# Quantising w_down in the attention stage of a gated cross-attention block, and transposing it by DMA from DRAM

## The chip, the cores and the metric

The kernel runs on one core of one Trainium2 chip. The metric is the device time of one execution in microseconds (us), as the median over runs: lower is better. Engines are named as in the profile: PE is TensorE's matmul, PEld its weight load, DVE VectorE, ACT ScalarE, POOL GpSimd, SP SyncE (which here only issues DMAs).

## What is computed

The block takes x (2 x 2048 x 512, f32) and a context of 2 x 77 x 384, and computes

```
x = x + tanh(g_xattn) * (softmax(q k^T * scale) v) Wo          # 16 heads of 32, q from layernorm(x)
xq = act_fake_quant(layernorm(x), clip_x)                      # one scale for the whole tensor
h = act_fake_quant(silu(xq wq(w_gate)^T) * (xq wq(w_up)^T), clip_down)   # 1408 hidden columns
x = x + tanh(g_ffn) * (h wq(w_down)^T)                         # w_down is 512 x 1408

wq(w) = clip(round(w / s), -128, 127) * s,  s = max(|w|, axis=1) / 127   # one scale per row of w
```

What matters here is the last weight. Row r of w_down (one of 512) gets its own scale, its 1408 values become int8, and these small integers are exact in bf16. TensorE needs them the other way round, with the 1408 hidden indices on the partitions: the tile `wdT`, 128 x 11 x 512 in bf16.

## The kernel before, in words

The 4096 rows of x are 32 tiles of 128 rows. Three stages (blocks) follow each other, with a barrier of all engines between them.

**Attention** is written as slots (`tile_slots`, 36 of them, slots 4 to 19 in a hardware loop). In slot n every engine runs a fixed order of pieces that belong to neighbouring tiles: scores of tile n, probabilities and outputs of tile n-1, the output projection (`project`) of tile n-2, the second layer norm of tile n-3, queries of tile n+2, the transpose of tile n+4 and so on. In slots 0 to 21 each slot also takes one block of 128 rows of w_gate or w_up (`NW` is 22): SP loads it into `w_in` (`rows`, line 323), DVE takes the absolute maximum (L632), its reciprocal (L641) and the int8 values (L649), POOL casts them to bf16 in `w_bf` (L404), and SP brings them transposed into `wgu` with a DMA transpose from SBUF to SBUF (`rows_transposed`, L316). After slot 21 SP has nothing left to do in this stage. The order on DVE inside a slot is: maximum of the first half of the scores (L570), residual add (L609), subtraction (L576), statistics (L623), low part of the transposed output (L599), then the piece of the weights (L632), `bn_aggr` (L635), outputs (L584, L589), second half of the scores (L570), int8 weights (L649), subtraction (L576), `xmax` (L659), low part of the queries (L555), outputs, statistics of tile n+6 and the low part of the transposed x (L548). PE's transpose of the output two tiles back (L846, `out_transpose`) waits for that low part (L548) of the slot before.

**Up** computes the hidden activations in 8 groups of 512 rows. A group has 11 steps (u counts them, 88 in all); a step is four matmuls of 128x512 for the gate and four for up (L1235), a silu on ACT (L1120), a product on DVE (L1192) and a maximum of it (L1196). The quantised inputs of the next group are made by ACT (L1095), cast by POOL (L1089) and transposed by SP's DMA transposes into `xqT` (L1064), four tiles to a group; `xqb`, the source, has two buffers, and POOL waits for the transpose of two tiles back before it writes one again. After a group is done, SP stores h of groups 0 to 3 to DRAM (`h_spill`, L1072, 2816 KB each) from the same queue.

In the first two groups every engine also has a piece of w_down. SP loads it as four blocks of 128 rows into the part of `h` that group 3 uses (L1057). In step u, `wd_step(u)` gives the block r (five steps each) and its phase k: DVE takes maxima (L1162), the scale (L1167, L1169, L1170) and int8 chunks of 512, 512 and 384 columns (L1177); ACT casts a chunk to bf16 one step later (L1106); PE transposes it, 4, 4 and 3 times 128x128, after the matmuls of a step (L1245); ACT copies the result from PSUM to `wdT` (L1112).

```
c = wd_chunk(u - 2) if isinstance(g, int) and g < 2 else None
if c is not None:
    pe.wait_ge(a_wdb, c + 1)          # ACT's cast of chunk c
    if c >= 2:
        pe.wait_ge(a_wdT, c - 1)      # ACT's copy of chunk c-2
```

**Down** multiplies the quantised h by `wdT`, 11 matmuls of 128x512 for each of 32 tiles (L1406).

Of the kernel before, what the change touches and what calls it, by code (L numbers as in the profile page):

```python
# [15 lines left out]
P = 128  # L16
# [35 lines left out]

CHUNKS = [(0, 4), (4, 8), (8, 2 * KB)]


def flamingo_block(nc, x, ctx_in, mask, g_xattn, g_ffn, Wq, Wk, Wv, Wo, clip_x, clip_down,
# [3 lines left out]
    h_spill = nc.dram_tensor("h_spill", [NS * TG, P, KI * P], F32, kind="Internal").ap()  # L60

    top = ExitStack()
    with top:
# [29 lines left out]
        with attn:  # L93
# [17 lines left out]
            with work:  # L111
# [26 lines left out]
                w_inv = sb("w_inv", [P, 1])  # L138

# [107 lines left out]
                v_wi8 = sem("v_wi8")  # L247
                a_xhi = sem("a_xhi")
# [61 lines left out]
                def _(sp):  # L310
# [218 lines left out]
                def _(dve):  # L529
# [70 lines left out]

                    def slot(n, t):
# [27 lines left out]
                        if runs(n, NW):  # L629
# [3 lines left out]
                               .then_inc(v_wam, 1)  # L633
                        if runs(m, NT):
# [11 lines left out]
                        if runs(n, NW):  # L646
# [3 lines left out]
                               .then_inc(v_wi8, 1)  # L650
                        if runs(n, NT):
# [5 lines left out]
                        if runs(n - 4, NT):  # L657
                            wait(dve, a_abs, n - 3)
                            dve.tensor_reduce(xmax[:, span(n - 4)], xabs[:, :], X, ALU.max).then_inc(v_xmax, 1)  # L659
                        if runs(n + 2, NT):  # L660
# [301 lines left out]
        with ffn:  # L962
# [10 lines left out]
            with up:  # L973
# [11 lines left out]
                wd_am = sb("wd_am", [P, KD, WC])  # L985
                wd_max = sb("wd_max", [P, KD])
                wd_inv = sb("wd_inv", [P, KD])
                wd_i8 = [sb(f"wd_i8{i}", [P, D], I8) for i in range(2)]
                wd_bf = [sb(f"wd_bf{i}", [P, D], BF16) for i in range(2)]

                wd_raw = h[:, (NS - 1) * TG:NS * TG, :, :].rearrange("p t k n -> p t (k n)")
                p_w = [pb(f"w{i}", [P, 2 * KD, P], BF16) for i in range(2)]
                l_wd = [sem(f"l_wd{i}") for i in range(KD)]
                v_wd = sem("v_wd")
                v_wd8 = sem("v_wd8")
                a_wdb = sem("a_wdb")
                t_wd = sem("t_wd")
                a_wdT = sem("a_wdT")
# [28 lines left out]
                def wd_cols(q):  # L1027
                    return slice(q * D, min(q * D + D, I))

                def wd_step(u):  # L1030
                    r, k = divmod(u, WC + 2)
                    return (r, k) if isinstance(u, int) and 0 <= r < KD else (None, None)

                def wd_chunk(u):

                    r, k = wd_step(u)
                    return r * WC + k - 2 if r is not None and k >= 2 else None

# [16 lines left out]
                def _(sp):  # L1055
                    for r in range(KD):
                        sp.dma_start(wd_raw[:, r, :], w_down[r * P:(r + 1) * P, :]).then_inc(l_wd[r], 16)  # L1057
                    def tiles_transposed(g):
                        if g >= 2:
                            sp.wait_ge(t_u, KI * (g - 1))  # L1060
                        for t in range(TG):
# [3 lines left out]
                              .then_inc(d_xqT[n % 2], 16)  # L1065

                    for g in range(1, NG):
                        tiles_transposed(g)
                        if g <= NG - NS:
# [4 lines left out]
                              .then_inc(h_out[f], 16)  # L1074
                    for i in range(2):
# [16 lines left out]
                def _(act):  # L1092
# [5 lines left out]
                    def down_part(u):  # L1098

                        c = wd_chunk(u - 1)  # L1100
                        if c is not None:
                            n = wd_cols(c % WC).stop - wd_cols(c % WC).start
                            act.wait_ge(v_wd8, c + 1)
                            if c >= 2:
                                act.wait_ge(t_wd, c - 1)
                            act.copy(wd_bf[c % 2][:, 0:n], wd_i8[c % 2][:, 0:n]).then_inc(a_wdb, 1)  # L1106
                        c = wd_chunk(u - 3)
                        if c is not None:
                            r, q = divmod(c, WC)
                            n = (wd_cols(q).stop - wd_cols(q).start) // P  # L1110
                            act.wait_ge(t_wd, c + 1)
                            act.copy(wdT[:, 4 * q:4 * q + n, r * P:(r + 1) * P], p_w[c % 2][:, 0:n, :])\  # L1112
                               .then_inc(a_wdT, 1)

                    def group(g, j, slot):
                        for i in range(KI):
# [7 lines left out]
                            if isinstance(g, int) and g < 2:  # L1124
                                down_part(u)
                        if isinstance(g, int) and g == 1:
                            down_part(2 * KI)
# [10 lines left out]
                def _(dve):  # L1138
# [16 lines left out]
                    def down_part(u):  # L1155
                        r, k = wd_step(u)
                        if r is None:
                            return
                        if k < 2:
                            dve.wait_ge(l_wd[r], 16)  # L1160
                            for q in ((0, 1), (2,))[k]:
                                dve.tensor_reduce(wd_am[:, r, q:q + 1], wd_raw[:, r, wd_cols(q)], X, ALU.max,  # L1162
                                                  apply_absolute_value=True).then_inc(v_wd, 1)
                        steps = (WC + 3) * r + WC
                        if k == 1:
                            dve.wait_ge(v_wd, steps)
                            dve.tensor_reduce(wd_max[:, r:r + 1], wd_am[:, r, :], X, ALU.max).then_inc(v_wd, 1)  # L1167
                            dve.wait_ge(v_wd, steps + 1)
                            dve.reciprocal(wd_inv[:, r:r + 1], wd_max[:, r:r + 1]).then_inc(v_wd, 1)  # L1169
                            dve.tensor_scalar(swd[:, r:r + 1], wd_max[:, r:r + 1], 1.0 / QMAX, None, ALU.mult)\  # L1170
                               .then_inc(v_wd, 1)
                        if k >= 2:
                            c, cols = wd_chunk(u), wd_cols(k - 2)
                            dve.wait_ge(v_wd, steps + 3)
                            if c >= 2:
                                dve.wait_ge(a_wdb, c - 1)
                            dve.tensor_scalar(wd_i8[c % 2][:, 0:cols.stop - cols.start], wd_raw[:, r, cols],  # L1177
                                              wd_inv[:, r:r + 1], QMAX, ALU.mult, ALU.mult).then_inc(v_wd8, 1)

                    def group(g, j, slot):  # L1180
# [6 lines left out]
                        for i in range(KI):  # L1187
# [10 lines left out]
                            if isinstance(g, int) and g < 2:  # L1198
                                down_part(u)
# [234 lines left out]
```

## Time and profile before

| | us |
|---|---|
| median of 3 runs (660.31 to 660.74) | 660.56 |
| the profiled execution, its own time | 660.23 |
| its span, from the first to the last instruction | 658.4 |
| attention, until the up stage's first instruction | 406.2 |
| up, from the first to the last start of four L1235 matmuls | 413.4 to 570.5 |
| down, from its first L1406 matmul to the end | 577.8 to 658.4 |

PE is busy 97% of the span, DVE 76%, ACT 50%, POOL 25%. The profile gives for each engine the start and length of its instructions, what ended the idle time ahead of them, and the clock that TensorE was granted. Matmuls overlap, so the length of one (379 ns) is not the time it costs; the distance between starts is. The row that a view prints for a run of the same matmuls begins with the start of the first.

### The profile page before, as it was taken

How to read it: one execution, taken by the hardware profiler on the slowest of the kernel's cores; microseconds unless marked ns; L12 is line 12 of the kernel's file. 1: busy time of each engine (PE TensorE's matmuls, PEld its weight loads, DVE VectorE, ACT ScalarE, POOL GpSimd, SP SyncE). 2: the span in 40 equal slices, each digit the busy share in tenths (PEclk: the TensorE clock that was granted, in tenths of full speed). 3: DMA queues.
4: the chain of work that ended last, by engine and by line, in shares of the span. 5: the costliest groups of instructions: out<-in, count | busy, mean ns of one | idle time of the engine just before them, and what ended most of it. 6: DMA issues, size and time to landing. Idle time of an engine off the chain costs nothing. (4 is left out here: it accounts for less than half of the span.)

```text
span 658.4 us, 12936 instructions
## 1 busy us (share of the span) xinstructions
PE 636.1 (97%) x4018; PEld 478.7 (73%) x4018; DVE 502.8 (76%) x942; ACT 330.7 (50%) x509; POOL 167.3 (25%) x378
## 2 busy tenths in 40 slices
PE   8979999999999999999999996999999999899997
PEld 6779999999999999999999994444444444444443
DVE  6687788787878878777776665899888888866664
ACT  5254545444554544445454344667555554265553
POOL 7121213232232323211100111111111110057775
PEclk9989999999999999999999997999999999999999
DMA  8739111111010101000000002343565110089623
GB/s 304 188 110 295 49 25 50 24 31 41 24 48 24 48 24 40 18 1 1 1 2 1 1 1 98 102 183 78 165 209 201 30 24 17 0 321 399 270 109 114
DMA packets 51079, 60.45 MB, mean 92 GB/s; under 512 B 33475, under 2 KB 33629, under 8 KB 51037
## 3 DMA queue, kind: packets, MB, share of 16 engines
q1 hardware_dynamic: 46131, 43.15, 21.8%
q10 hardware_dynamic: 4906, 16.78, 6.9%
q8 instruction: 22, 0.36, 0.2%
q14 instruction: 20, 0.16, 0.1%
HBM read 32.48 MB, written 19.92 MB: 80 GB/s over the span
## 5 line engine op out<-in xcount | busy, mean ns | idle before, releaser
L570 DVE TENSOR_REDUCE sb_smax<-ps_s 128x8 f32<-128x616 f32 x64 | 51.1, 799 | 66.7 <-PE ps_s L801 66.5
L1235 PE MATMUL ps_g<-sb_xqT,sb_wgu 128*128 128x512 bf16 x352 | 90.4, 379 | 0.6 <-DVE sb_xqT L1203 0.5
L1235 PE MATMUL ps_u<-sb_xqT,sb_wgu 128*128 128x512 bf16 x352 | 90.3, 379 | 0.0
L1120 ACT ACTIVATE sb_silu<-ps_g,sb_sgu 128x512 f32<-128x512 f32 x88 | 60.5, 687 | 59.2 <-PE ps_g L1235 30.9
L464 ACT COPY sb_pT<-ps_p 128x512 f32<-128x512 f32 (+1 forms) x96 | 46.4, 520 | 70.6 <-PE ps_p L812 70.6
L823 PE MATMUL ps_o<-sb_vblk,sb_pT 128*128 (+4 forms) x640 | 79.0, 270 | 1.2 <-ACT sb_pT L464 1.2
L823 PEld LDWEIGHTS ps_o<-sb_vblk,sb_pT 128*128 128x128 f32 (+1 forms) x640 | 76.8, 191 | 1.8 <-ACT sb_pT L464 1.4
L756 PE MATMUL ps_q<-sb_xT_hi,sb_wq_hi 128*128 128x256 f32 x256 | 77.5, 303 | 0.0
L1192 DVE SCALAR_TENSOR_TENSOR sb_h<-ps_u,sb_sgu,sb_silu 128x512 f32<-128x512 f32 (+1 forms) x88 | 65.9, 749 | 14.9 <-PE ps_u L1235 13.1
L1406 PE MATMUL ps_z<-sb_wdT,sb_hq 128*128 128x512 bf16 x352 | 76.4, 380 | 0.0
L758 PE MATMUL ps_q<-sb_xT_hi,sb_wq_lo 128*128 128x256 f32 x256 | 72.3, 282 | 0.0
L757 PE MATMUL ps_q<-sb_xT_lo,sb_wq_hi 128*128 128x256 f32 x256 | 72.2, 282 | 0.0
L1318 POOL TENSOR_TENSOR sb_wgu<-sb_wgu,sb_x 128x512 f32<-128x512 f32 x31 | 53.9, 1737 | 53.2 <-DVE sb_wgu L1363 53.2
L1196 DVE TENSOR_REDUCE sb_hmax<-sb_h 128x1 f32<-128x512 f32 (+1 forms) x88 | 60.4, 686 | 7.6
L1406 PEld LDWEIGHTS ps_z<-sb_wdT,sb_hq 128*128 128x128 bf16 x352 | 34.4, 98 | 42.3 <-ACT sb_hq L1333 0.8
L1235 PEld LDWEIGHTS ps_u<-sb_xqT,sb_wgu 128*128 128x128 bf16 x352 | 34.4, 98 | 41.5 <-DVE sb_h L1192 0.5
L452 ACT CAST sb_oT_hi<-ps_x 128x512 fp32r<-128x512 f32 x31 | 18.2, 586 | 90.7 <-PE ps_x L846 90.7
L1235 PEld LDWEIGHTS ps_g<-sb_xqT,sb_wgu 128*128 128x128 bf16 x352 | 33.8, 98 | 39.5 <-DVE sb_xqT L1203 0.7
L1333 ACT CAST sb_hq<-sb_h 128x1408 bf16<-128x1408 int8 x32 | 43.6, 1365 | 35.1 <-DVE sb_h L1357 35.1
L576 DVE TENSOR_TENSOR sb_prob<-ps_s,sb_smax 128x616 f32<-128x616 f32 x64 | 51.0, 797 | 3.0
L386 POOL TENSOR_TENSOR sb_ve<-sb_mvt,sb_eps 128x1 f32<-128x1 f32 x32 | 6.1, 190 | 180.0 <-DVE sb_mvt L635 180.0
L756 PE MATMUL ps_y<-sb_wo_hi,sb_oT_hi 128*128 128x512 f32 x124 | 51.3, 414 | 0.0
(177 smaller groups left out, 1348.5 us busy)
## 6 DMA issues: line engine op xcount, KB each, us to landing
h_spill<-sb_h SPq DMA_DIRECT2D x4, 2816.0 KB, 8.8
sb_h<-h_spill ACTq DMA_DIRECT2D x16, 704.0 KB, 6.5
out_dram<-sb_wgu SPq DMA_DIRECT2D x32, 256.0 KB, 2.1
sb_x<-in_x_dram ACTq DMA_DIRECT2D x1, 4096.0 KB, 18.3
sb_w_in<-in_L_ffn_w_gate_dram SPq DMA_DIRECT2D x11, 256.0 KB, 2.6
sb_w_in<-in_L_ffn_w_up_dram SPq DMA_DIRECT2D x11, 256.0 KB, 2.7
sb_h<-in_L_ffn_w_down_dram SPq DMA_DIRECT2D x4, 704.0 KB, 6.0
sb_x<-in_x_dram SPq DMA_DIRECT2D x2, 1024.0 KB, 14.8
```

The costliest lines, as they stand in the source:

```text
L570: dve.tensor_reduce(smax[:, half, :].rearrange("p (g h) -> p g h", g=2), half_scores(), X, ALU.max).then_inc(v_max, 1)
L576: dve.tensor_tensor(prob[t % 2][:, half, :].rearrange("p (g h m) -> p g h m", g=2, h=HG), half_scores(), smax[:, half, :].rearrange("p (g ...
L756: pe.matmul(o, hi, rhi, start=first, stop=False)
L757: pe.matmul(o, hi, rlo, start=False, stop=False)
L758: return pe.matmul(o, lo, rhi, start=False, stop=last)
L823: last = pe.matmul(p_o[:, first:end + 1, :].rearrange("p h d -> p (h d)"), pT[rows, half * KB + j, :], vblk[rows, span(b), half, SLOT0[j]: ...
L1120: act.activation(silu[(j * KI + i) % 2][:, :, :].rearrange("p t n -> p (t n)"), p_g[(j * KI + i) % 2][:, :], ACT.Silu, scale=sgu[:, i:i + ...
L1192: dve.scalar_tensor_tensor(steps_h, p_u[(j * KI + i) % 2][:, :, :], sgu[:, KI + i:KI + i + 1], silu[(j * KI + i) % 2][:, :, :], ALU.mult, ...
L1196: dve.tensor_reduce(hmax[:, span(u)], steps_h, mybir.AxisListType.XY, ALU.max, apply_absolute_value=True).then_inc(v_hmax, 1)
L1235: last = pe.matmul(banks[(j * KI + i) % 2][:, :], wgu[:, what, k, i * P:(i + 1) * P], xqT[j][:, k, :], start=(k == 0), stop=(k == KD - 1))
L1318: pool.tensor_tensor(yd[k], yd[k], x1[:, span((v + RT) % NT), :].rearrange("p a d -> p (a d)"), ALU.add).then_inc(g_out, 1)
L1406: last = pe.matmul(p_z[k % 4][:, :], hq[k % 4][:, i, :], wdT[:, i, :], start=(i == 0), stop=(i == KI - 1))
```

## The change

w_down leaves the up stage. In attention slots 22 to 29 two slots go to each block r of 128 rows: in the even one DVE takes the three maxima and the scale, in the odd one it makes the int8 chunks. POOL casts chunks 0 and 1 in the odd slot and chunk 2 in the next one, into the one buffer `w_bf`, and SP stores each to `wd_spill` in DRAM. The raw rows lie in `w_in`, in a new tile `w_in2` and in `vblk` of batch 0, which is free once that batch's outputs are done (`t_o`). In the up stage SP issues, after tiles 1 and 3 of groups 1 and 2, one DMA transpose of a 128 x 1408 block from DRAM into `wdT`. The pieces on PE, ACT and DVE of the up stage, the four loads and their PSUM tiles are gone.

```diff
+    wd_spill = nc.dram_tensor("wd_spill", [KD, P, I], BF16, kind="Internal").ap()
...
+                w_in2 = sb("w_in2", [P, I - 2 * D])
+                vb0 = vblk[:, 0, :, :, :].rearrange("p a s d -> p (a s d)")
+                wd_in = [w_in[:, :], vb0[:, 0:D], w_in2[:, :]]
+                wd_i8 = [w_i8[:, :], vb0[:, D:D + D // 4].bitcast(I8), vb0[:, D + D // 4:D + D // 2].bitcast(I8)]
...
@@ attention, SP, after rows_transposed(NW - 1)
+                    def down_rows(r):
+                        if r:
+                            sp.wait_ge(v_wd8, WC * r)
+                        for q in range(WC):
+                            cols = wd_cols(q)
+                            sp.dma_start(wd_in[q][:, 0:cols.stop - cols.start], w_down[r * P:(r + 1) * P, cols])\
+                              .then_inc(l_wd[r], 16)
+
+                    def down_stored(r, q):
+                        cols = wd_cols(q)
+                        sp.wait_ge(g_wdb, WC * r + q + 1)
+                        sp.dma_start(wd_spill[r, :, cols], w_bf[:, 0:cols.stop - cols.start]).then_inc(d_wdb, 16)
+
+                    sp.wait_ge(t_o, 2 * (S // P))
+                    sp.wait_ge(v_wi8, NW)
+                    down_rows(0)
+                    for r in range(KD):
+                        for q in range(WC - 1):
+                            down_stored(r, q)
+                        if r + 1 < KD:
+                            down_rows(r + 1)
+                        down_stored(r, WC - 1)
                     sp.wait_ge(d_wT, 16 * NW)
+                    sp.wait_ge(d_wdb, 16 * KD * WC)
@@ attention, POOL, at the end of slot(n, t)
+                        for m, parts in ((n - 1, [WC - 1]), (n, range(WC - 1))):
+                            r, k = wd_step(m)
+                            for q in parts if k == 1 else []:
+                                c, size = WC * r + q, wd_cols(q).stop - wd_cols(q).start
+                                pool.wait_ge(v_wd8, c + 1)
+                                wait(pool, d_wdb, 16 * c)
+                                if c == 0:
+                                    pool.wait_ge(d_wT, 16 * NW)
+                                pool.tensor_copy(w_bf[:, 0:size], wd_i8[q][:, 0:size]).then_inc(g_wdb, 1)
@@ attention, DVE: down_part(n, 0) ahead of L635, down_part(n, 1) ahead of the second L576,
@@ down_part(n, 2) and down_scale(n) ahead of L555
+                    def down_part(n, q):
+                        r, k = wd_step(n)
+                        if k == 0:
+                            if q == 0:
+                                dve.wait_ge(l_wd[r], 16 * WC)
+                            dve.tensor_reduce(wd_am[:, r, q:q + 1], wd_in[q], X, ALU.max,
+                                              apply_absolute_value=True).then_inc(v_wdam, 1)
+                        if k == 1:
+                            if q == 0:
+                                dve.wait_ge(v_wds, 3 * r + 3)
+                                dve.wait_ge(g_wbf, NW)
+                                wait(dve, g_wdb, WC * r)
+                            size = wd_cols(q).stop - wd_cols(q).start
+                            dve.tensor_scalar(wd_i8[q][:, 0:size], wd_in[q][:, 0:size], wd_inv[:, r:r + 1], QMAX,
+                                              ALU.mult, ALU.mult).then_inc(v_wd8, 1)
@@ up, SP
-                    for r in range(KD):
-                        sp.dma_start(wd_raw[:, r, :], w_down[r * P:(r + 1) * P, :]).then_inc(l_wd[r], 16)
                     def tiles_transposed(g):
...
                             sp.dma_start_transpose(xqT[g % 2][:, :, t * P:(t + 1) * P], xqb[n % 2][:, :])\
                               .then_inc(d_xqT[n % 2], 16)
+                            if g <= KD // 2 and t % 2:
+                                r = (g - 1) * 2 + t // 2
+                                sp.dma_start_transpose(wdT[:, :, r * P:(r + 1) * P], wd_spill[r]).then_inc(d_wdT, 16)
...
+                    sp.wait_ge(d_wdT, 16 * KD)
@@ up, PE (ACT's down_part with L1106 and L1112, and DVE's with L1162 to L1177, go as well)
-                            c = wd_chunk(u - 2) if isinstance(g, int) and g < 2 else None
-                            if c is not None:
-                                pe.wait_ge(a_wdb, c + 1)
-                                if c >= 2:
-                                    pe.wait_ge(a_wdT, c - 1)
-                                for k in range((wd_cols(c % WC).stop - wd_cols(c % WC).start) // P):
-                                    last = pe.transpose(p_w[c % 2][:, k, :], wd_bf[c % 2][:, k * P:(k + 1) * P],
-                                                        identb[:, :])
-                                last.then_inc(t_wd, 1)
```

`wd_step(n)` in attention gives block `(n - 22) // 2` and phase `(n - 22) % 2`; `down_scale(n)` makes the block's maximum, its reciprocal and `swd` in phase 0, three instructions of one column or three, each waiting for the one before.

## Rows read from the trace of the kernel before

**Rows 1.** Two windows: busy us (count) of PE, PEld, DVE, ACT, POOL; clock, DMA, GB/s
```profile
254.40:265.90 11.50, 11.50 (x88) 10.98 (x87) 9.38 (x20) 5.77 (x10) 2.88 (x11) 1.00 0.15 36
413.40:457.40 44.00, 41.51 (x220) 19.01 (x220) 40.88 (x78) 30.53 (x53) 4.91 (x8) 1.00 0.36 102
```

**Rows 2.** Timeline of PE, attention (start us, us, then engine, line, operation, count)
```profile
254.38 0.30 PE L799 MATMUL ps_s<-sb_k_hi,sb_q_hi 128*128 128x308 f32 x1
255.24 0.60 PE L846 MATMUL ps_x<-sb_identf,sb_o_sb 128*128 128x128 f32 x4
265.89 0.30 PE L799 MATMUL ps_s<-sb_k_hi,sb_q_hi 128*128 128x308 f32 x1
...
288.90 0.30 PE L799 MATMUL ps_s<-sb_k_hi,sb_q_hi 128*128 128x308 f32 x1
300.40 0.30 PE L799 MATMUL ps_s<-sb_k_hi,sb_q_hi 128*128 128x308 f32 x1
```

**Rows 3.** Timeline of PE, up stage
```profile
413.36 1.04 PE L1235 MATMUL ps_g<-sb_xqT,sb_wgu 128*128 128x512 bf16 x4 [0.52 <-DVE sb_xqT L1203]
...
422.72 0.40 PE L1245 MATMUL ps_w<-sb_identb,sb_wd_bf 128*128 128x128 bf16 x4 [0.55 <-ACT sb_wd_bf L1106]
422.95 1.03 PE L1235 MATMUL ps_g<-sb_xqT,sb_wgu 128*128 128x512 bf16 x4
...
424.90 1.03 PE L1235 MATMUL ps_g<-sb_xqT,sb_wgu 128*128 128x512 bf16 x4
...
457.42 1.03 PE L1235 MATMUL ps_g<-sb_xqT,sb_wgu 128*128 128x512 bf16 x4
...
569.66 1.03 PE L1235 MATMUL ps_g<-sb_xqT,sb_wgu 128*128 128x512 bf16 x4
```

**Rows 4.** Timeline of DVE, attention, slot 20 (it has a weight block)
```profile
258.77 0.68 DVE L632 TENSOR_REDUCE sb_w_am<-sb_w_in 128x1 f32<-128x512 f32 x1
...
260.87 0.48 DVE L649 TENSOR_SCALAR sb_w_i<-sb_w_in,sb_w_inv 128x512 int8<-128x512 f32 x1
...
264.16 0.68 DVE L548 TENSOR_TENSOR sb_xT_lo<-ps_x,sb_xT_hi 128x512 fp32r<-128x512 f32 x1
```

**Rows 5.** Timeline of DVE, up stage, the pieces of block 0
```profile
416.69 1.27 DVE L1162 TENSOR_REDUCE sb_wd_am<-sb_h 128x1 f32<-128x512 f32 x2
417.88 0.74 DVE L1192 SCALAR_TENSOR_TENSOR sb_h<-ps_u,sb_sgu,sb_silu 128x512 f32<-128x512 f32 x1
...
419.25 0.54 DVE L1162 TENSOR_REDUCE sb_wd_am<-sb_h 128x1 f32<-128x384 f32 x1
...
420.15 0.74 DVE L1192 SCALAR_TENSOR_TENSOR sb_h<-ps_u,sb_sgu,sb_silu 128x512 f32<-128x512 f32 x1
```

**Rows 6.** Timeline of SP's queue: the last weight transpose, two input transposes of up
```profile
273.75 1.19 SPq L316 DMA_TRANSPOSE sb_wgu<-sb_w_bf  x1
...
419.98 1.19 SPq L1064 DMA_TRANSPOSE sb_xqT<-sb_xqb  x1
...
464.04 2.11 SPq L1064 DMA_TRANSPOSE sb_xqT<-sb_xqb  x1
```

**Rows 7.** All of L1064: issue ns min/median/max, time to landing; loads of the page
```profile
L1064 SPq DMA_TRANSPOSE sb_xqT<-sb_xqb x28: 1189/1192/2729, 416.6 to 546.9; - x28
...
DMA to landing us min/median/max: 2.4/2.5/8.3
...
sb_w_in<-in_L_ffn_w_up_dram SPq DMA_DIRECT2D x11, 256.0 KB, 2.7
```

**Rows 8.** DMA of 270 to 280 us (one transpose): packets, MB, share of 16 engines
```profile
q1 hardware_dynamic: 544, 0.13, 6.7%
```

**Rows 9.** DMA of 262 to 264.45 us (one 256 KB load, one transpose), same columns
```profile
q1 hardware_dynamic: 688, 0.39, 64.7%
```

**Rows 10.** PE between up and down: us, busy (x), granted clock, DMA share, GB/s
```profile
575.00:576.00 1.00, 1.00 (x6) 0.53 0.00 0
...
578.00:579.00 1.00, 1.00 (x5) 0.77 0.91 338
```

More of the change, by code:

```diff
@@ L51, with wd_cols, wd_step @@
 ROWS = [min(P, HW - P * k) for k in range(KB)]
+WD0 = 2 * KI
+def wd_cols(q):
+    return slice(q * D, min(q * D + D, I))
+def wd_step(n):
+    r, k = divmod(n - WD0, 2) if isinstance(n, int) else (-1, 0)
+    return (r, k) if 0 <= r < KD else (None, None)
 CHUNKS = [(0, 4), (4, 8), (8, 2 * KB)]
@@ L138, in flamingo_block @@
                 w_inv = sb("w_inv", [P, 1])
+                wd_am = sb("wd_am", [P, KD, WC])
+                wd_max = sb("wd_max", [P, KD])
+                wd_inv = sb("wd_inv", [P, KD])
+                w_in2 = sb("w_in2", [P, I - 2 * D])
+                vb0 = vblk[:, 0, :, :, :].rearrange("p a s d -> p (a s d)")
+                wd_in = [w_in[:, :], vb0[:, 0:D], w_in2[:, :]]
+                wd_i8 = [w_i8[:, :], vb0[:, D:D + D // 4].bitcast(I8), vb0[:, D + D // 4:D + D // 2].bitcast(I8)]
                 p_s = pb("s", [P, 2, 512])
@@ L247, in flamingo_block @@
                 v_wi8 = sem("v_wi8")
+                l_wd = [sem(f"l_wd{r}") for r in range(KD)]
+                v_wdam = sem("v_wdam")
+                v_wds = sem("v_wds")
+                v_wd8 = sem("v_wd8")
+                g_wdb = sem("g_wdb")
+                d_wdb = sem("d_wdb")
                 a_xhi = sem("a_xhi")
@@ L599, in out_part, with down_scale @@
                         dve.tensor_tensor(o_lo, p_x[:, :, :], o_hi.bitcast(F32), ALU.subtract).then_inc(v_olo, 1)
+                    def down_part(n, q):
[13 more added lines that the diff above has]
+                                              ALU.mult, ALU.mult).then_inc(v_wd8, 1)
+                    def down_scale(n):
+                        r, k = wd_step(n)
+                        if k == 0:
+                            dve.wait_ge(v_wdam, WC * (r + 1))
+                            dve.tensor_reduce(wd_max[:, r:r + 1], wd_am[:, r, :], X, ALU.max).then_inc(v_wds, 1)
+                            dve.wait_ge(v_wds, 3 * r + 1)
+                            dve.reciprocal(wd_inv[:, r:r + 1], wd_max[:, r:r + 1]).then_inc(v_wds, 1)
+                            dve.tensor_scalar(swd[:, r:r + 1], wd_max[:, r:r + 1], 1.0 / QMAX, None, ALU.mult)\
+                               .then_inc(v_wds, 1)
                     def slot(n, t):
@@ L633, in slot @@
                                .then_inc(v_wam, 1)
+                        down_part(n, 0)
                         if runs(m, NT):
@@ L650, in slot @@
                                .then_inc(v_wi8, 1)
+                        down_part(n, 1)
                         if runs(n, NT):
@@ L659, in slot @@
                             dve.tensor_reduce(xmax[:, span(n - 4)], xabs[:, :], X, ALU.max).then_inc(v_xmax, 1)
+                        down_part(n, 2)
+                        down_scale(n)
                         if runs(n + 2, NT):
@@ L984, in flamingo_block @@
                 sgu = sb("sgu", [P, 2 * KI])
[L985 to L998, printed above, removed]
+                d_wdT = sem("d_wdT")
                 rsq = sb("rsq", [P, NT])
@@ L1022, in flamingo_block @@
                 v_hmax = sem("v_hmax")
[L1027 to L1037, printed above, removed]
                 def groups(eng, group):
@@ L1123, in group @@
                                 quantise(g * TG + TG + i // 2, i // 2)
[L1124 to L1127, printed above, removed]
                     act.activation(warm[:, :], eps[:, :], ACT.Silu).then_inc(a_warm, 1)
@@ L1153, in _ @@
                     dve.wait_ge(v_sx, 5)
[L1155 to L1178, printed above, removed]
                     def group(g, j, slot):
@@ L1197, in group @@
                                               apply_absolute_value=True).then_inc(v_hmax, 1)
-                            if isinstance(g, int) and g < 2:
-                                down_part(u)
                     def place(n):
```

15 lines of the change are left out of this document (removed).

## The prediction

> **What bounds the kernel now.** I read the windows first. In a slot of the attention stage PE is busy for all 11.50 us and DVE for 9.38; in groups 0 and 1 of the up stage PE is busy for 41.5 of 44 us, DVE for 40.9 [rows 1]. So PE sets the pace in both places, and the second is the only long stretch in which it has gaps. Whether PE is bound by itself or by someone it waits for is read from its timeline, from the distance between starts.
>
> Attention: the first scores matmul of slot 20 starts at 254.38, of slot 21 at 265.89, of slot 23 at 288.90, of slot 24 at 300.40 [rows 2]. Which slot is which follows from SP: the last of 22 weight transposes is issued at 273.75, so that slot is number 21 [rows 6]. A slot takes 11.50 us with a weight block and without one. DVE's and POOL's share of the weight costs nothing there; that cover is what the change leans on.
>
> Up: group 2 starts at 457.42 and its last step's gate at 569.66, 65 steps later [rows 3]. That is 1.7268 us a step, eight matmuls of 216 ns, with no room in between. The first 22 steps should take 22 x 1.7268 = 37.99 us; they take 457.42 - 413.36 = 44.06. **The w_down pieces cost PE 6.07 us**, and PE is the bound behind them, so this is on the path. One gap shows what it is made of: the four transposes start at 422.72 after 0.55 us of idle time that ACT's cast ends, the gate matmuls follow at 422.95, and the next chunk, whose cast is ready, makes the step 424.90 - 422.95 = 1.95 us, 0.22 more than a plain one [rows 3]. The rest is waiting for ACT, which waits for DVE.
>
> **The change, part by part.**
>
> Removed from PE: the transposes and the waits ahead of them, 6.07 us, all of it. What is late next in groups 0 and 1? DVE: its 40.9 us [rows 1] lose the w_down pieces. They take 1.19 us for two maxima (416.69 to 417.88) and 0.90 for the third and the scale (419.25 to 420.15) [rows 5], and three int8 chunks of up to 0.48 each, as L649 takes [rows 4]: about 3.5 us a block, 14 in all. 27 us are left for 38 us of PE. ACT also loses work. So the pace becomes that of group 2 onward, which the trace shows PE holding for 65 steps. I take the whole 6.07.
>
> Added to DVE in attention, even slots 22 to 28: 1.19 + 0.90 = 2.09 us [rows 5], against 0.68 + 0.48 = 1.16 and a small reciprocal in a slot with a weight block [rows 4]. That is some 0.9 us more than DVE is known to hide. Who waits? The tightest is PE's L846 in the next slot, 0.86 us after that slot's start (255.24 - 254.38) [rows 2], so at 266.75 for slot 21; it needs L548 of slot 20, which ends at 264.16 + 0.68 = 264.84 [rows 4]. The slack is 1.9 us; 0.9 goes, 1.0 is left. Odd slots add three int8 chunks, at most 1.44 us, 0.3 above a weight slot: hidden. In the last two slots, 28 and 29, DVE has less of its own to do. POOL has 2.88 of 11.5 us busy [rows 1]; its two casts in a slot and its wait for each store queue only the layer norm of a later tile behind them. Cost nothing; the bounds are nothing and, if every one of the eight slots lost the 0.3 us by which my estimates could err, 2.4 us.
>
> The loads: SP issues block 0 after 273.75 + 1.19 = 274.94; three loads at 2.7 us to landing each [rows 7], three in a row at most 8. DVE wants them in slot 22, whose start is 265.89 + 11.50 = 277.39, at the place of L632, 258.77 - 254.38 = 4.39 us into it: 281.8 [rows 2, 4]. Landed by then, by 283 at the worst, and L548's slack covers the 1.2. Later blocks have more: SP issues them when the odd slot's chunks are done. The twelve stores and the wait for them end some 30 us before the stage does. Nothing.
>
> Gone from the start of up: four loads of 704 KB that nobody waited for in time. Nothing.
>
> **The four DMA transposes** are the unknown. No row shows a source in DRAM or 1408 columns. Issue on SP: 1.19 us for 512 columns [rows 7], so between 1.19 (if it is a fixed price) and, with the longest that a busy queue makes of it (2.73), 2.73 x 2.75 = 7.5 us; I take 1.19 x 2.75 = 3.3, the uncontended rate. Transfer: 6.7% of 10 us = 0.67 us for 512 columns [rows 8], so 1.84 us from below. From above: a 256 KB load and a transpose together take 64.7% of 2.45 us = 1.59 [rows 9], so the load's 128 packets take 0.92 us, 115 ns each on one of 16 engines; were each of the 1408 pieces as slow, 88 x 0.115 = 10.1 us. I take about 2.5, near the transposes' own row.
>
> One rule of the Trainium skill says that this is a bargain: by "Advanced Engine Details and Errata", section "X-Bar Transpose (TRN2)", a DMA transpose is as fast as a plain DMA, 350 to 400 GB/s. By that estimate the 360 KB would take 1.0 us; the trace speaks against it, 0.131 MB in 0.67 us is 196 GB/s [rows 8], and the sum goes by the row.
>
> What stands behind them? SP's queue is in order, so tiles 2 and 3 of the same group are issued after the first of the pair. Group 0: tile 1's issue ends at 419.98 + 1.19 = 421.17 [rows 6]; with X for the issue of a block, tiles 2 and 3 need 1.19 each and 1.3 more to land (2.5 in all [rows 7]), 421.17 + X + 3.68. Group 1 now starts at 413.36 + 11 x 1.7268 = 432.36. Free up to X = 7.5. Group 1: here the 2.8 MB store of h goes through the same queue. The pattern of group 2, undisturbed by w_down, gives tile 1's issue ended 464.04 + 2.11 - 457.42 = 8.73 us after the start [rows 3, 6], so 12.41 + X against 19.0: free up to X = 6.6. With X = 3.3 the slack is 4.2 and 3.3 us. Blocks 1 and 3 follow tile 3 and end before the next store is due. Nothing.
>
> **Down.** The granted clock is 0.5 of full, the 1.2 GHz level, from 575.06 to 578.46 [rows 10], after the pause between the stages. The down matmuls start at 577.83, so 0.63 us at half speed cost 0.3. Moved by 6 us, the stretch may miss them (0.3 less) or fall wholly on them (3.4 / 2 = 1.7, 1.4 more). I put nothing into the sum.
>
> **Sum.** Profiled execution: 660.23 - 6.07 = 654.16, span 652.4. The median shown stands 0.33 above that execution, so 660.56 - 6.07 = **654.5**.
>
> **Rivals.**
> (a) *The transposes from DRAM hold up the input tiles a little.* X between 6.6 and 8, or their transfer in the upper half of its bounds. For it: in group 1 the queue is already slow (2.11, 2.73, a landing of 8.3 us [rows 6, 7]). Against: X would be over twice the rate of the rows. It gives back 1 to 4 us: 655.5 to 658.5.
> (b) *They hold it up much*: the slower side. The mechanism is SP's queue. Four blocks in a row delay tiles, then the store of h, then group 2's tiles: with X the tiles of group 2 land at 432.0 + 3X (block 0, tiles 2 and 3, block 1, store, tiles 0 and 1 at 2.2 each, block 2, tiles 2 and 3), against 451.4. That is 3X - 19.4 late, and eats the 6.07 from X = 8.5 us on; at X = 10, the same as the upper bound of the transfer, it is 10.6 late: 665.1. A sentence of the Trainium skill points that way: "DMA: Bandwidth & Descriptors", section "Why small descriptors are slow (HBM only)", says that short descriptors pay on HBM and not between SBUF tiles. The rows here show only the SBUF kind [rows 8].
> (c) *DVE's even slots overrun.* If maxima and scale take 1 us longer than in up, or the loads come late, L846 waits: four to eight slots by 0.3 us, 655.7 to 656.9. Against: 1.0 us of slack.
> (d) *The low clock falls on the down stage*: 655.9.
> (e) *Nothing moves*: another engine holds groups 0 and 1 at 2 us a step. Against it stand the 65 steps after them. 660.5.
>
> **How the numbers follow.** Forecast 0.70; (a) 0.07, (b) 0.08, (c) 0.06, (d) 0.06, (e) 0.03. A measurement of this kernel tells 0.2%, 1.3 us, from no change. All but (b) and (e) are faster: 0.89; (e) is the same, 0.03; (b) slower, 0.08. The range goes from 653.6 (the clock's 0.3 and the scatter of the runs, 0.4, below the sum) to 657.2, which takes in (c), (d) and half of (a): 0.15 lies outside.
>
> **What would show it.** Group 1's gate should start 19.0 us after group 0's and group 2's 38.0 us after, no L1245 or L1106 in up; slots 22 to 27 keep 11.50 us and 28 and 29 their length; L548 in even slots about 1 us later. Block transposes: issue near 3.3 us, landing within 6. The prediction is wrong if PE idles ahead of group 1 or 2 for a transpose, or if a slot of 22 to 29 is longer than before.

## The result, and the profile after

The changed kernel takes 655.62 us (median of 7 runs, 652.95 to 657.17) beside 660.7 us of the kernel before (7 runs, 658.95 to 662.6) on the same chip: ratio 0.992, 95% interval 0.9894 to 0.9945. A second measurement gave 653.86 us (6 runs) beside 660.23 (11 runs), ratio 0.9902 [0.9882, 0.9921]. The forecast was 654.5 in 653.6 to 657.2: faster, and both medians are inside. The profiled execution of after took 652.95 us with a span of 651.1, that of before 660.23 and 658.4. The difference of 7.28 us is 6.06 in groups 0 and 1 of the up stage, 1.01 ahead of it (413.36 - 412.35), and 0.2 behind.

Four windows of the changed kernel: a slot of attention that takes the maxima and the scale of a w_down block (slot 22), a slot that makes the int8 chunks (23), the first two groups of the up stage, and groups 2 on. [rows 1] has a slot and the two groups of the kernel before. Columns: us, busy us (count) of PE, PEld, DVE, ACT, POOL; granted clock; DMA share; GB/s.

```profile
276.33:287.84 11.51, 11.51 (x87) 10.99 (x86) 10.25 (x23) 5.76 (x10) 1.34 (x6) 1.00 0.11 38
287.84:299.34 11.50, 11.50 (x87) 10.98 (x86) 9.77 (x22) 5.77 (x10) 3.64 (x13) 1.00 0.12 32
412.35:450.35 38.00, 38.00 (x177) 17.23 (x178) 30.17 (x42) 20.69 (x30) 4.90 (x8) 1.00 0.57 142
450.35:563.50 113.15, 113.15 (x526) 51.30 (x525) 94.03 (x131) 58.68 (x86) 12.27 (x20) 1.00 0.31 100
```

DVE took on work in attention, 10.25 of 11.51 us busy where [rows 1] has 9.38, and PE is still busy for the whole slot. In up, DVE's count is 42 where it was 78, and PE has no gap left in 38.00 us. The starts behind it, from PE's timeline of the up stage:

```profile
412.35 1.04 PE L1258 MATMUL ps_g<-sb_xqT,sb_wgu 128*128 128x512 bf16 x4 [0.52 <-DVE sb_xqT L1226]
...
431.35 1.03 PE L1258 MATMUL ps_g<-sb_xqT,sb_wgu 128*128 128x512 bf16 x4
...
450.35 1.03 PE L1258 MATMUL ps_g<-sb_xqT,sb_wgu 128*128 128x512 bf16 x4
```

Group 1 begins 19.00 us and group 2 38.00 us after group 0, where [rows 3] have 44.06 for the second. This is one execution; in a second profiled execution of the same kernel the 38.00 are 39.28 (below, on the clock). The blocks arrive through SP's queue. Its timeline in the up stage (start us, issue us), and then all four of L1135 and all 28 of L1131, the input's transposes, with issue ns min/median/max:

```profile
418.97 1.19 SPq L1131 DMA_TRANSPOSE sb_xqT<-sb_xqb  x1
420.21 1.42 SPq L1135 DMA_TRANSPOSE sb_wdT<-wd_spill  x1
...
427.11 1.44 SPq L1135 DMA_TRANSPOSE sb_wdT<-wd_spill  x1
432.33 0.40 SPq L1142 DMA_DIRECT2D h_spill<-sb_h  x1
434.55 5.52 SPq L1131 DMA_TRANSPOSE sb_xqT<-sb_xqb  x2
440.12 2.82 SPq L1135 DMA_TRANSPOSE sb_wdT<-wd_spill  x1
444.15 2.50 SPq L1131 DMA_TRANSPOSE sb_xqT<-sb_xqb  x2
446.70 1.45 SPq L1135 DMA_TRANSPOSE sb_wdT<-wd_spill  x1
```

```profile
L1135 SPq DMA_TRANSPOSE sb_wdT<-wd_spill x4: 1422/1444/2821, 420.2 to 446.7; - x4
...
DMA to landing us min/median/max: 3.6/3.7/4.8
```

```profile
L1131 SPq DMA_TRANSPOSE sb_xqT<-sb_xqb x28: 1189/1191/2177, 415.6 to 539.8; - x28
```

A block costs SP 1.42 us, hardly more than the 1.19 of an input tile with 2.75 times fewer columns: nearly a fixed price. Only the third, issued some 8 us behind the 2.8 MB store of h, costs twice that, 2.82. The last input tile that is issued during group 1 is issued by 446.65, and group 2, which reads it, starts at 450.35.

In attention the question was L611, the subtraction of the low part of x that PE waits for in the next slot. DVE's timeline at the end of slot 22, and PE's around the start of slot 23:

```profile
284.71 0.54 DVE L669 TENSOR_REDUCE sb_wd_am<-sb_w_in 128x1 f32<-128x384 f32 x1
...
287.21 0.68 DVE L611 TENSOR_TENSOR sb_xT_lo<-ps_x,sb_xT_hi 128x512 fp32r<-128x512 f32 x1
...
288.89 0.80 DVE L633 TENSOR_REDUCE sb_smax<-ps_s 128x8 f32<-128x616 f32 x1 [0.91 <-PE ps_s L894]
```

```profile
287.84 0.30 PE L892 MATMUL ps_s<-sb_k_hi,sb_q_hi 128*128 128x308 f32 x1
...
288.69 0.38 PE L939 MATMUL ps_x<-sb_identf,sb_o_sb 128*128 128x128 f32 x2
```

L611 ends at 287.89 and PE comes to L939 at 288.69: 0.8 us are left, and DVE still sits idle for 0.91 us afterwards. Every slot from 22 to 27 lasts 11.50 us and slots 28 and 29 last 11.1, as before.

### The profile page after: what moved, and what is told of

It reads as the page before. It is cut to its first block and busy times, and to the rows that moved or that the text cites. A ratio compares the mean times of both kernels' runs of the same rounds, so it can differ in the third digit from the quotient of the medians.

```text
span 651.1 us, 12848 instructions
## 1 busy us (share of the span) xinstructions
PE 630.8 (97%) x3974; PEld 475.6 (73%) x3974; DVE 502.3 (77%) x942; ACT 320.0 (49%) x485; POOL 173.7 (27%) x390
```

## The experiments

Ten kernels ran, in three batches; the kernel before took 660.2, 660.37 and 660.23 us in them (medians of 22, 25 and 11 runs). Eight take the change apart, the others repeat it and extend it. Times are medians.

**What held groups 0 and 1 back.** The prediction put the 6.07 us on PE's transposes and on PE's wait for ACT's cast. In the kernel before, this edit moves the transposes of a chunk between the gate and the up matmuls of the next step, 0.86 us later:

```
 last.then_inc(done, 1)
+if what == 0 and isinstance(g, int) and g < 2:
+    down_chunk(wd_chunk(u - 3))       # was wd_chunk(u - 2), after the step
```

> The kernel before, with PE's w_down transposes moved from the end of a step to between the next step's gate and up matmuls, 0.86 us later. Nothing else is changed. Theory (6.07 us are 2.4 us of PE work and 3.6 us of waiting for ACT's cast, which was up to 0.64 us late): the waits go, the work stays, group 2 starts 38.0 + 2.4 = 40.4 us after group 0 and the kernel takes about 656.9, 3.6 less than before. Rival (the whole 6.07 is the price of the transposes' work on PE, switching included): group 2 still starts 44 us after group 0, 660.5.

Measured: 660.63 us (10 runs), ratio 1.0007 [0.9989, 1.0025]. Groups 0 and 1 take 457.54 - 413.50 = 44.04 us, as before. PE's timeline in the up stage, two of its gaps:

```profile
431.20 0.39 PE L1246 MATMUL ps_u<-sb_xqT,sb_wgu 128*128 128x512 bf16 x1 [0.38 <-DVE sb_h L1192]
...
441.30 0.39 PE L1246 MATMUL ps_u<-sb_xqT,sb_wgu 128*128 128x512 bf16 x1 [0.38 <-DVE sb_h L1192]
```

These gaps of PE were not closed, they became waits for DVE's h, which frees the PSUM bank. The two stand 10.10 us apart, five steps at 2.02 us. The theory of the wait for ACT fell. The new one: DVE, busy 40.9 of 44 us [rows 1], sets the pace, and whoever PE asks next is late. DVE's timeline of the kernel before bears it out. The pairs of maxima that open blocks 1 and 2:

```profile
426.79 1.27 DVE L1162 TENSOR_REDUCE sb_wd_am<-sb_h 128x1 f32<-128x512 f32 x2
...
436.89 1.27 DVE L1162 TENSOR_REDUCE sb_wd_am<-sb_h 128x1 f32<-128x512 f32 x2
```

With that of block 0 at 416.69 [rows 5] they are 10.10 us apart, and from its first h at 415.30 until 457.5 DVE's timeline shows no idle time ahead of any instruction. Two kernels each keep one half. The first is the changed kernel with PE's transposes and ACT's copies put back, but with blocks loaded ready from DRAM, so that DVE has no work for w_down in up and ACT has no casts:

```
-    sp.dma_start_transpose(wdT[:, :, r * P:(r + 1) * P], wd_spill[r])
+    sp.dma_start(wd_raw[:, r, 0:I], wd_spill[r])           # at the start of up, r = 0..3
+    last = pe.transpose(p_w[c % 2][:, k, :], wd_raw[:, c // WC, q * P:(q + 1) * P], identb[:, :])
+    act.copy(wdT[:, 4 * q:4 * q + n, r * P:(r + 1) * P], p_w[c % 2][:, 0:n, :])
```

> The changed kernel, but w_down comes back from DRAM with four plain loads and is transposed as before by PE (44 transposes after the steps of groups 0 and 1, L1245 of the kernel before) and copied by ACT. So PE and ACT have their work of before in up, and DVE has none. Theory after e1 (DVE is what paces groups 0 and 1 before the change: 10.1 us for every five steps; PE's own work is 44 transposes of 55 ns): group 2 starts 38.0 + 2.4 = 40.4 us after group 0, the kernel takes 2.4 us more than the changed one, about 657 to 658. Rival (the transposes cost PE the whole 6.07): 44 us, 660 to 661.

Measured: 656.64 us (10 runs), ratio 0.9945 [0.9926, 0.9964]. PE's timeline at both ends of groups 0 and 1:

```profile
413.82 1.04 PE L1278 MATMUL ps_g<-sb_xqT,sb_wgu 128*128 128x512 bf16 x4 [0.52 <-DVE sb_xqT L1246]
...
454.28 1.03 PE L1278 MATMUL ps_g<-sb_xqT,sb_wgu 128*128 128x512 bf16 x4
```

The distance is 40.46 us, so PE's transposes alone, with ACT's copies, cost 2.46. The other half is the kernel before without PE's transposes, ACT's casts and its copies; DVE's pieces stay, and wdT holds zeros, so the down product is left out of the output.

```
-    act.copy(wd_bf[c % 2][:, 0:n], wd_i8[c % 2][:, 0:n])
-    last = pe.transpose(p_w[c % 2][:, k, :], wd_bf[c % 2][:, k * P:(k + 1) * P], identb[:, :])
-    dve.wait_ge(a_wdb, c - 1)
+    pool.memset(wdT[:, n - TG, :], 0.0)                    # eleven small pieces
```

> The kernel before with DVE's w_down pieces in up, and without PE's transposes and ACT's casts and copies; GpSimd fills wdT with zeros between its casts, so the output is not the reference's. Theory (DVE paces groups 0 and 1): group 2 starts 42.5 to 44 us after group 0, against 44.06 before, and the kernel stays at 659 to 660.5, although all of PE's part is gone. Rival (the cost is PE's and ACT's): 38.0 us, about 654.5.

Measured: 659.02 us (10 runs), ratio 0.9972 [0.9954, 0.999]. The window of groups 0 and 1 (columns as above), one of PE's gaps, and two pairs of DVE's maxima:

```profile
413.40:457.40 44.00, 40.05 (x177) 16.27 (x180) 40.98 (x78) 20.71 (x30) 8.52 (x16) 1.00 0.38 108
```

```profile
429.71 1.04 PE L1231 MATMUL ps_u<-sb_xqT,sb_wgu 128*128 128x512 bf16 x4 [0.65 <-DVE sb_h L1188]
```

```profile
437.83 1.27 DVE L1160 TENSOR_REDUCE sb_wd_am<-sb_h 128x1 f32<-128x512 f32 x2
...
447.93 1.27 DVE L1160 TENSOR_REDUCE sb_wd_am<-sb_h 128x1 f32<-128x512 f32 x2
```

Groups 0 and 1 take 456.61 - 413.94 = 42.67 us: with nothing of w_down on PE or ACT they are still 4.67 us too long, DVE is busy for 40.98 us, and its blocks are 10.10 us apart as in the kernel before. (Some 0.35 us of the 4.67 are the filling's own: one int8 chunk, at 423.89, took 0.83 us instead of 0.48 beside a fill of POOL.) 2.46 and 4.67 make 7.13, more than the 6.06 of both: they overlap. Taking off PE's and ACT's work only would have saved 1.4 us, taking off DVE's, and with it ACT's casts, only 3.6.

**Do the additions cost anything?** The changed kernel without any of the w_down work (loads, maxima, casts, stores, block transposes); the down product is again left out.

```
-    down_part(n, 0)   (and 1, 2, down_scale, down_rows, down_stored, the casts)
-    sp.dma_start_transpose(wdT[:, :, r * P:(r + 1) * P], wd_spill[r])
+    pool.memset(wdT[:, :, :], 0.0)
```

> The changed kernel with everything of w_down left out: no loads, maxima, int8, casts, stores or block transposes; wdT is filled with zeros and swd with ones by GpSimd at the start of up, so the output is not the reference's. Theory (all that the change adds is hidden): the same as the changed kernel on the same chip, within its scatter of 653 to 657, slots 22 to 29 of 11.50 and 11.1 us, group 2 starts 38.0 us after group 0. Rival (the additions in attention or the block transposes cost something that the gain covered): faster by over 1 us, slots 22 to 29 shorter than the changed kernel's.

Measured: 659.69 us (10 runs), ratio 0.9986 [0.9968, 1.0004], slower than the changed kernel with all its work. The fill that should have cost nothing spoiled the run. Timelines of POOL, DVE and PE at the start of up:

```profile
405.97 4.79 POOL L1114 MEMSET sb_wdT<- 128x5632 bf16 x1
...
406.10 4.74 DVE L1153 TENSOR_SCALAR sb_spread<-sb_identf,sb_am 128x128 f32<-128x128 f32 x1
...
410.98 0.55 PE L1235 MATMUL ps_u<-sb_spread,sb_ones 128*128 128x128 f32 x1 [4.11 <-DVE sb_spread L1153]
```

DVE's small instruction lasted as long as POOL's fill (in the next kernel, without that fill beside it, it took 0.28 us), and up began at 417.34 instead of near 413. So it was done again with the fill in eleven pieces between POOL's casts, `pool.memset(wdT[:, n - TG, :], 0.0)`:

> e2 again with the filling of wdT cut in 11 pieces between GpSimd's casts (in e2 the one fill of 4.8 us held up DVE at the start of up). w_down is left out altogether; the output is not the reference's. Theory: the same as the changed kernel, 653 to 657, group 2 starts 38.0 us after group 0. Rival: the additions cost something, and it is faster than 652.5.

Measured: 655.5 us (5 runs), ratio 0.9931 [0.9904, 0.9959]. Up starts at 413.43, group 2 at 451.43: 38.00 us. The changed kernel, with all the work, has ratios of 0.992 and 0.9902: no difference that the runs can show, and its slots and its 38.00 us are the same. What it adds is hidden.

How well, is asked by two more. The maxima of the even slots are taken twice, 1.64 us more of DVE in each:

```
 dve.tensor_reduce(wd_am[:, r, q:q + 1], wd_in[q], X, ALU.max, apply_absolute_value=True)
+dve.tensor_reduce(wd_am2[:, r, q:q + 1], wd_in[q], X, ALU.max, apply_absolute_value=True)
```

> The changed kernel with each of the maxima of slots 22, 24, 26 and 28 taken twice, 1.7 us more of DVE in each of these slots. The trace of the changed kernel has 0.9 us of idle time left on DVE at the end of slot 22. Theory (the slack of the even slots is about 0.8 to 0.9 us): slots 22, 24 and 26 are longer by 0.6 to 1 us each, 28 by less since it has less other work, PE idle ahead of L939's transpose for L611; 2 to 3 us in all. Rival (DVE's queue has more give than that, since the lateness is made up in the odd slots): every slot keeps 11.50 us.

Measured: 657.45 us (7 runs), ratio 0.9945 [0.9927, 0.9963]. PE's timeline at the start of slot 23 and of slot 24, PE's waits from 200 to 400 us (us in total, times, longest), and DVE's timeline at the same start:

```profile
287.68 0.30 PE L895 MATMUL ps_s<-sb_k_hi,sb_q_hi 128*128 128x308 f32 x1
...
289.19 0.63 PE L942 MATMUL ps_x<-sb_identf,sb_o_sb 128*128 128x128 f32 x4 [0.49 <-issue]
...
299.86 0.30 PE L895 MATMUL ps_s<-sb_k_hi,sb_q_hi 128*128 128x308 f32 x1
```

```profile
PEld ps_x L942 <- DVE sb_o_sb L653: 1.4, 2, 0.7
```

```profile
288.41 0.68 DVE L612 TENSOR_TENSOR sb_xT_lo<-ps_x,sb_xT_hi 128x512 fp32r<-128x512 f32 x1
```

Slot 23 lasts 12.18 us, and so does 25 (323.54 - 311.36); slot 27 is 0.26 longer, slot 29 not at all: 1.6 us together where 2 to 3 were expected. 1.64 added, 0.68 of it came through in slots 23 and 25: the slack was 0.96 us. PE's transpose (L942) waits for two pieces of DVE, the outputs (L653) and the low part of x (L612). The view puts the wait down to L653, but that one ends at 288.49; L612 ends at 289.09, and PE goes on at 289.19. It is the instruction that the prediction named, L548 there. Next, the queue. In a copy of the changed kernel the block after tile 1 is transposed again and waited for each time, so that SP is held for about 8 us in each of the two groups; a further kernel does it three times, about 12 us:

```
 sp.dma_start_transpose(wdT[:, :, r * P:(r + 1) * P], wd_spill[r]).then_inc(d_wdT, 16)
+if t == 1:
+    for e in range(1):                                     # range(2) in the second
+        sp.wait_ge(d_wdT, ...)
+        sp.dma_start_transpose(wdT[:, :, r * P:(r + 1) * P], wd_spill[r]).then_inc(d_wdT, 16)
+    sp.wait_ge(d_wdT, ...)
```

> The changed kernel with SP's queue held up on purpose: after tile 1 of groups 1 and 2 the block is transposed twice and SP waits for the landing of each, so the time between tile 1 and tile 2 is X = 7.4 us (2 x 3.7) in group 0's time and about 8.5 us in group 1's, in place of 1.4 and 2.8. Theory (the input tiles are late from X = 7.5 us in group 0 and 6.6 in group 1): group 1 on time or 0.1 us late, group 2 about 1.5 to 2 us late, PE idle ahead of it for a transpose. Rival (POOL's buffers or ACT, not SP's queue, set when the tiles land): PE has no gap at all.

Measured: 656.51 us (5 runs), ratio 0.9947 [0.9921, 0.9973]. SP is held 7.5 us in group 0 and 8.6 in group 1. Group 1 is 0.16 us late; group 2, counted from group 1, is 2.3 us late, in PE's timeline:

```profile
452.63 0.39 PE L1264 MATMUL ps_g<-sb_xqT,sb_wgu 128*128 128x512 bf16 x1 [2.14 <-DMA sb_xqT<-sb_xqb]
```

The prediction's bounds, 7.5 and 6.6 us, ask for 0 and 8.6 - 6.6 = 2.0.

> As e3, with three transposes of each block, each waited for: X is about 11.1 us in group 0's time and 12 in group 1's. Theory: group 1 is late by 11.1 - 7.5 = 3.6 us, group 2 by some 5 to 6 more, since the store of h is late too; the kernel is 9 us slower than the changed one, about 664, slower than before. Rival: the store of h gives its lateness back and group 2 is late by under 3 us, the kernel stays under 661.

Measured: 667.62 us (2 runs), ratio 1.0114 [1.0076, 1.0151]. SP is held 11.2 and 11.5 us; PE's timeline at the start of groups 1 and 2, and the granted clock behind each gap (PE's windows: us, busy, clock, DMA share, GB/s):

```profile
436.77 0.59 PE L1264 MATMUL ps_g<-sb_xqT,sb_wgu 128*128 128x512 bf16 x1 [3.73 <-issue]
...
463.31 0.60 PE L1264 MATMUL ps_g<-sb_xqT,sb_wgu 128*128 128x512 bf16 x1 [4.48 <-DMA sb_xqT<-sb_xqb]
```

```profile
437.00:443.00 6.00, 6.00 (x16) 0.53 1.04 364
463.30:467.00 3.70, 3.69 (x10) 0.56 1.05 332
```

Group 1 comes 436.77 - 413.88 = 22.89 us after group 0 instead of 19.00, group 2 26.54 after group 1: 11.4 us late together. The bounds ask for 11.2 - 7.5 = 3.7 and 11.5 - 6.6 = 4.9; the first was 3.9 and the second 7.5. Of the second 2.9 us are PE at the 1.2 GHz level: without a pause it comes to the last four matmuls of group 1 (457.80) 21.03 us after the group's start, where the changed kernel takes 18.14. That leaves 4.6, near the bound. The expectation, about 664, had no such term. The slower side was real, at four to eight times the hold that the kernel has.

**The clock at 46 us.** The 1.01 us ahead of up was in no term of the sum. PE's windows of before (first fence) and after (second), same columns:

```profile
46.00:48.00 2.00, 2.00 (x9) 0.50 0.91 285
48.00:50.00 2.00, 2.00 (x14) 0.65 0.99 329
```

```profile
46.00:48.00 2.00, 1.43 (x12) 1.00 0.89 287
48.00:50.00 2.00, 2.00 (x20) 1.00 0.92 318
```

Before ran at 1.2 GHz here and after at 2.4, and nothing of the change is near. From the end of a pause that both have to the scores that open slot 4, before needs 70.54 - 45.77 = 24.77 us, after 69.48 - 45.64 = 23.84: that is 0.93 of the 1.01. The pause, in before's timeline of PE, and in after's:

```profile
45.77 0.46 PE L799 MATMUL ps_s<-sb_k_hi,sb_q_hi 128*128 128x308 f32 x1 [1.75 <-DVE sb_q_lo L555]
```

```profile
45.64 0.41 PE L892 MATMUL ps_s<-sb_k_hi,sb_q_hi 128*128 128x308 f32 x1 [1.74 <-DVE sb_q_lo L618]
```

DVE is late there because slot 1 also holds a subtraction of 2.39 us, that of Wo's low part (L746 of after). Two kernels ran together, the changed one again, and one in which that subtraction stands behind the pieces that PE waits for:

```
-                        if isinstance(n, int) and n == 1:
-                            dve.wait_ge(a_wo, 1)
-                            dve.tensor_tensor(wo_lo[:, :, :], wo_raw, ..., ALU.subtract).then_inc(v_wo, 1)
                         ...
                             x_part(n + 4, t)
+                        if isinstance(n, int) and n == 1:   (the same three lines)
```

> The changed kernel itself, more runs of it: its times lie between 652.95 and 657.17 where the clock's low stretches fall otherwise from run to run. Theory: median 655 to 656; the profile again shows 38.0 us from group 0 to group 2 and slots of 11.50 us, and what differs from the first profile lies where the granted clock is low. Rival: part of the scatter is in the block transposes, and group 1 or 2 starts late in this profile.

> The changed kernel with one piece of DVE moved: in slot 1 the subtraction for wo_lo (2.4 us, L746) goes behind the low parts of the queries and of x. In the changed kernel PE is idle 1.74 us for L618 behind it at 43.9 us, and in the profile of the kernel before the granted clock is 0.58 in the 4 us after that pause, but 1.00 in the profile of the changed one. Theory: the pause goes, slot 2 starts 1.7 us earlier and no execution has a low clock there: 1.7 us faster in all, 2.7 in those that had it, median 653 to 654, scatter under 3 us. Rival: what DVE now does first does not help, since its queue is full there and the lateness turns up in slot 2: the same as the changed kernel.

Measured: the changed kernel 653.86 us (6 runs, 652.63 to 655.62), the other 652.63 (6 runs, 651.16 to 654.61), ratio to before 0.9886 [0.9867, 0.9906]. PE's windows of the changed kernel's repeat, then the other's timeline of PE and its window:

```profile
46.00:48.00 2.00, 1.44 (x12) 0.93 0.86 292
48.00:50.00 2.00, 2.00 (x11) 0.50 0.99 341
50.00:52.00 2.00, 2.00 (x15) 0.72 1.06 382
```

```profile
44.13 0.41 PE L892 MATMUL ps_s<-sb_k_hi,sb_q_hi 128*128 128x308 f32 x1
```

```profile
46.00:50.00 4.00, 4.00 (x36) 1.00 0.88 287
```

The same kernel that kept its clock in one profiled execution lost it in another, 2 us later than before did. And it lost it a second time, at the start of up. PE's timeline and window there, in the repeat:

```profile
413.73 1.89 PE L1258 MATMUL ps_g<-sb_xqT,sb_wgu 128*128 128x512 bf16 x4 [0.52 <-DVE sb_xqT L1226]
...
453.01 1.03 PE L1258 MATMUL ps_g<-sb_xqT,sb_wgu 128*128 128x512 bf16 x4
```

```profile
413.00:415.00 2.00, 1.48 (x7) 0.50 0.03 8
```

Groups 0 and 1 take 39.28 us here, not the 38.00 that were expected again. PE has no pause in them and no transpose is late; the granted clock is 0.50 to 415 and 0.66 in the next 2 us, and the steps behind that take 1.727 us again. Up starts 1.38 us later than in after's profile and groups 0 and 1 take 1.28 longer: together 2.66, the whole difference between 655.61 and 652.95. The profiles of the doubled maxima and of the kernel with the one fill have the same low stretch at the start of up (39.41 and 39.69 us for groups 0 and 1). Of the eleven profiled executions with this pause (before, after and the first nine kernels) eight show the low clock behind it; after and the kernels with the 8 us hold and the doubled maxima do not. With the pause gone (no idle time ahead of 44.13) the clock stays and up starts at 410.82. The medians are 1.2 us apart, less than the 1.7 or more expected, the runs of the two overlap, and this kernel's own spread is 3.45 us where under 3 was expected: the pause is not the only source of the scatter. This kernel has the lowest median of all, below both kernels of this case.

## Why the prediction was right, and where its steps were not

**The sum.** 6.07 us off groups 0 and 1, nothing added: the starts give 6.06 and nothing, and 4.78 in the second profile, where the clock is low at the start of up. (A span of 658.4 - 6.07 is 652.3, not 652.4; nothing hangs on it.) The medians fell by 5.1 and 6.4 us. The runs of either kernel scatter over some 4 us; the 0.4 that the range allowed for them was too small.

**Groups 0 and 1.** The size was right, since it was read as the difference from 65 undisturbed steps. The step that failed is the one behind it: "The w_down pieces cost PE 6.07 us, and PE is the bound behind them". The first experiment moves PE's work and nothing changes, and either half alone is 2.46 or 4.67. DVE paced five steps in 10.10 us, with PE's w_down work and without it. The prediction saw 41.5 us busy on PE and 40.9 on DVE and took the larger for the bound; what told them apart was idle time, which PE had and DVE had not. The forecast survived because the change takes the work off both. As far as this step goes that is luck: had the change taken off PE's and ACT's work alone, the same step would have promised 6.07 us where the runs show 1.4. DVE is left with 30.17 us busy, not 27: its pieces were sized a little too high.

**Attention.** Slack of "1.9 us; 0.9 goes, 1.0 is left": 0.96 by the longer slots, 0.8 to 0.9 by the rows. The doubled maxima show the wait that was named: PE's transpose of the outputs goes on when the low part of x ends, not at L653, which the view of waits gives. Loads: the first was issued at 274.00, the up stage starting 1.01 us earlier in this execution (forecast 274.94), and DVE waited for none in slots 22 to 29. Rival (c) did not occur.

**SP's queue.** Issue taken as 3.3 us from 1.19 x 2.75: 1.42. Of the two ends the fixed price was nearly right, and the choice went to the wrong one; nothing hung on it, because the limits of 7.5 and 6.6 us, confirmed by the 8 us kernel, are far off. Transfer taken as 2.5 us: the window from 419 to 427 us holds the data of one block and of two input tiles (2528 packets, 0.62 MB, 37.4% of 8 us = 2.99 us), less 2 x 0.67 [rows 8] leaves 1.65, below the 1.84 taken as the lower end. Per packet, DRAM as a source was no slower than SBUF: 1440 packets in 1.65 us, 544 in 0.67. Rival (a) did not occur. Rival (b) is a true mechanism (11.5 us of hold makes the kernel slower than before), but its formula 3X - 19.4 is not borne out. That kernel holds the queue at blocks 0 and 2 alone, for 11.2 and 11.5 us, and block 1 took 1.4; in place of 3X these make 24.1, 4.7 us late, where 11.4 was lost. The formula lets the queue run without a pause. In the trace SP waited there for POOL's casts of the next inputs, 3.3 and 3.5 us in group 1, since those are made as the group goes on. The bounds by group, 7.5 and 6.6, count from each group's start; they and the clock account for the 11.4.

**The clock.** The low stretch ahead of down missed the down matmuls in after's profile: the granted clock is 0.50 to 570.5 and 0.86 in the next half us, and they start at 570.89. That is the "0.3 less" of the prediction, which it left out of the sum. The 1.0 us at 46 us and the 1.28 at the start of up were on no list. Rival (d) did not occur. Rival (e), another engine at 2 us a step, was true of the kernel before, DVE at 2.02; it did not occur in the changed one, since DVE's work went with PE's.

What stays open: why the clock falls at the same place in one execution and not in the next. It accounts for the 2.66 us between the two profiled executions of the changed kernel; for the rest of the scatter of 4 us no profile here tells.

## What to carry to other kernels

Size a saving from an undisturbed stretch of the same loop, not from the gaps and the engine that the profile names beside them: a wait ended by one engine may be the shadow of another, and moving work on the first then brings nothing. The engine that sets the pace is the one whose own timeline has no idle time, at the same period when the other's work is taken away. Before work is moved into a full stage, count the slack to the one instruction that the bound engine asks for next; here 0.96 us were left, and 1.64 us more cost 0.68 a slot. In a queue that works in order, work out how long a new transfer may hold it; then the transfer's unknown price matters only beyond that. And before a difference of a us or two is explained, profile the same kernel twice: here two executions of one kernel differed by 2.66 us in the clock alone.

## What the runs showed of the hardware

A DMA transpose costs its queue nearly a fixed time: 1.19 us for 128x512 bf16, 1.42 for 128x1408, 2.82 some 8 us behind a 2.8 MB store in the same queue. From DRAM it moved 360 KB in 1.65 us, 218 GB/s, and 131 KB between SBUF tiles in 0.67 us, 196 GB/s [rows 8]. The Trainium skill, "Advanced Engine Details and Errata", section "X-Bar Transpose (TRN2)", gives 350 to 400 GB/s; the runs show little over half of it. The block's small packets did not cost more from DRAM than from SBUF, where the Trainium skill, "DMA: Bandwidth & Descriptors", section "Why small descriptors are slow (HBM only)", would have them do.

Beside a POOL memset of 128x5632 bf16 (4.79 us) a DVE tensor_scalar of 128x128 lasted 4.74 us, and 0.28 us without it. The Trainium skill, "SBUF — State Buffer", section "Who interferes with whom", says that the two engines share one pair of ports, that a tensor_scalar of DVE can enter a mode that needs it, and that the first to issue then holds the pair for its whole instruction while the other is blocked. The trace agrees: DVE started 0.13 us after POOL and ended 0.08 us after it.

A pause of 1.75 us in otherwise full work was followed by some 3.5 us at the 1.2 GHz level in eight of the eleven profiled executions that have it, and not in the other three; the same kernel did the one in one execution and the other in the next. At the start of up some 2.6 us at the low level (granted clock 0.50 from 413.73 to 415, 0.66 in the next 2 us) cost that kernel 1.28 us.
